# A gated cross-attention and feed-forward kernel: the first batch's value rows cast straight into their stack, W's centring split anew, the context product by parts of W, and the last two tiles reordered

## The chip, the core and the metric

The kernel runs on one core of one Trainium2 chip. The metric is the device time of one execution, in microseconds. Before the change the median of 3 runs is 316.41 us (316.31 to 316.99).

## The reference

x is (4, 2048, 512), the context c is (4, 77, 512), everything float32. LN is a layer norm without weights (eps 1e-5).

```python
scores = einsum('bsd,bvd->bsv', LN(x), c)          # 4 x 2048 x 77
x1  = x  + tanh(g_xattn) * einsum('bsv,bvd->bsd', softmax(scores), c)
Wl  = W + up_aux @ (lora_up @ (lora_down @ down_aux))   # 512 x 512, low-rank part
out = x1 + tanh(g_ffn) * (einsum('bsi,oi->bso', LN(x1), Wl) + b)
```

## The kernel before, in words

The 8192 rows of x are worked as 64 tiles of 128 rows, 16 to a batch. Since LN is linear up to a row's scale, x1's product with W is never made from x1: it is x times W (centred over its input) plus P times (c times W), so that one set of products serves. Tensors of weights are in two parts, a rounded "hi" and a "lo" remainder, each in the type fp32r, and a product is the sum of three such products (hi hi, hi lo, lo hi).

`wc` holds W's two parts (512 columns) and beside them the centred context's columns (77), so that one product of a tile's transposed x (`xT`, hi and lo) gives both x times W and the scores. `x_product` (L502) makes it in halves: h=1 is the wide half with the scores (334 columns), h=0 the other (256). Both halves are 4 chunks of 3 products each. `stacks` holds for a batch the value rows: columns 0 to 511 are tanh(g) c, columns 512 to 1023 the context product tanh(g) c W. Its hi and lo rows stand under each other in the partitions (77 hi rows at 0, 13 lo rows at 77, 13 hi rows again at 96; in a second plane 64 hi rows at 0 and 64 lo rows at 64), in such an order that P's transposed parts (`pT`) times the stack is again the sum of hi and lo products. `p_product` (L518) makes a_ps (P times c, which with x gives x1) and adds P times (c W) to `y_ps`.

For a tile t, in each engine's own order written out by hand (`step`, run for t = 0 to 64 by `all_tiles`):
- TensorE (L540): first chunk of t's wide half, P transpose of tile t-1, the rest of the wide half and half of h=0, `p_product` of t-1, the rest of h=0.
- VectorE (L692): maxima of t, output of t-2, inverse of the exponents' sum of t, x1 rows and mean of t-1, row statistics of t+2, lo parts of P of t.
- ScalarE (L410): hi parts of P of t-1, exponents of t, hi part of x of t+2, probabilities of t, variance of x1 of t-1.
- GpSimd (L300): bias added to x1 of t-1, the two reciprocal roots, lo part of x of t+2.
- SyncE (L232): stores a pair of tiles ("unit") once both are out and loads the unit four further.

The start, before tile 0: TensorE multiplies identities (`stay_busy`, L465) between its first tasks: 12, then the low-rank input product (L473), 4, the context's transposes (L482), the low-rank output product (L566), 6, then the transposes of W rows 0 and 1 with 4 behind each, and at last rows 2 and 3 with the low-rank product L582 into the same banks. W's four blocks of 128 rows are centred first: blocks 0 and 1 on VectorE (L719 to L725), block 2 on ScalarE (L436, L442), block 3 on GpSimd (L330) with the mean of ScalarE. `wc` is then filled by ScalarE (hi, L452) and VectorE (lo, L741), chunk by chunk; the context product (L497, 12 products into a_ps) follows them chunk by chunk. Its result goes to `v_hi` (ScalarE, L358) and `v_lo` (VectorE, L621), and by five SBUF to SBUF copies into the stack: three from SyncE's queue (`stack_hi`, L221) and two from ScalarE's (`stack_lo`, L201, called at L457). TensorE waits for all five (L525) before P's first product. SyncE issues the loads of units 1 and 2 ahead of these copies and those of unit 3 behind them. Batches 1 to 3 are prepared in the same way inside the tile loop, with both kinds of copies on SyncE's queue.

At the end, step 64 has only P's transpose and `p_product` of tile 63 on TensorE; the last unit is stored tile by tile (L270 to L273).

Of the kernel before, what the change touches and what calls it, by code (L numbers as in the profile page):

```python
# [19 lines left out]
def build_kernel(nc, x, xt_in, ctx_in, W, b_gates, low_in, low_out, out):  # L20
# [17 lines left out]
    DMAS = 5  # L38
    assert TB == 2 * HB and V + R <= 96 and D == 512
# [4 lines left out]
    with ExitStack() as stack:  # L44
# [56 lines left out]
        squares = sb("squares", [P, D])  # L101
# [19 lines left out]
        def p_transposed(k):  # L121
            return y_half(k, 0)[:, H:H + P]
# [35 lines left out]
        expd_ok = sem("expd_ok")  # L158
# [6 lines left out]
        def all_tiles(step, prep):  # L165

            for t in range(T + 1):
# [23 lines left out]

        def unit_turn(t, k, ring):

            return t // ring
# [5 lines left out]

        def stack_lo(eng, n):  # L201

            eng.wait_ge(v_lo_ok, 2 * n + 2)
            lo, to = v_lo[:, :].bitcast(F32), stacks[:, n % 2, :, :].bitcast(F32)
            for rows, source in ((to[V:V + R, 0, :], lo[Q:V, :]), (to[Q:P, 1, :], lo[0:Q, :])):
                eng.dma_start(rows, source).then_inc(stacked[n % 2], 16)

        @block.sync
        def _(sp):
# [11 lines left out]
            def stack_hi(n):  # L221
# [5 lines left out]
                sp.wait_ge(v_hi_ok, 2 * n + 2)  # L227
                hi, to = v_hi[:, :].bitcast(F32), stacks[:, n % 2, :, :].bitcast(F32)
                for rows, source in ((to[0:V, 0, :], hi), (to[96:K0, 0, :], hi[Q:V, :]), (to[0:Q, 1, :], hi[0:Q, :])):
                    sp.dma_start(rows, source).then_inc(stacked[n % 2], 16)  # L230
# [18 lines left out]
            sp.dma_start(b_row[:, 0:D], b_gates[0:D].partition_broadcast(P)).then_inc(ld_b, 16)  # L249
            sp.wait_ge(ld_x[0], 16)  # L250
            for u in range(1, 3):
                load_xt(u, u)
                load_x(u, u)
            stack_hi(0)
            load_xt(3, 3)
            load_x(3, 3)
            NU = TB // UNIT
            for u in range(B * NU - 1):
                n, k = u // NU, u % NU
                if n < B - 1:  # L260
# [4 lines left out]
                    if k == NU - 2:  # L265
                        stack_hi(n + 1)
                        stack_lo(sp, n + 1)
# [10 lines left out]
        def _(pool):  # L278
# [15 lines left out]
            def x_lo(t, k):  # L294

                pool.wait_ge(xh_ready, t + 1)
# [3 lines left out]
            def step(t, k):  # L300
# [12 lines left out]
                if t == -2:  # L313
                    first_columns()
                q, a, b = (k + 2) % 4, 0 if real(t + 2) else 1, 2 if real(t - 1) else 1
# [10 lines left out]
            def prep(n, k):  # L326
                pass

            pool.wait_ge(w_nmean_ok, 2)
            pool.tensor_scalar(w_cent[:, 3, :], w_rows[:, 3, :], w_nmean[:, 1:2], None, ALU.add)\  # L330
                .then_inc(w_centred[3], 1)
# [5 lines left out]
        def _(act):  # L337
            act.dma_start(c_rows[:, :], ctx_in[0]).then_inc(ld_ctx, 16)
# [3 lines left out]
            act.dma_start(b_row[:, D:D + 2], b_gates[D:D + 2].partition_broadcast(P)).then_inc(ld_gates, 16)  # L342
# [3 lines left out]
            def ctx_rows_hi(n):  # L346
# [4 lines left out]
                else:  # L351
                    act.wait_ge(stacked[(n - 1) % 2], 16 * DMAS * ((n - 1) // 2 + 1))
# [50 lines left out]
            def variance(t, k):  # L403
# [3 lines left out]
                act.activation(squares[:, :], x1[:, k % 2, :], ACT.Square, bias=x1_nmean[:, k % 2:k % 2 + 1],  # L407
                               scale=D ** -0.5, accum_out=stat[:, s, 2:3]).then_inc(var1_ready, 1)

            def step(t, k):  # L410
                if real(t - 1):
                    p_hi(t - 1, k - 1)
                if switches(t, SWITCH):
# [7 lines left out]
                if real(t - 1):  # L421
# [5 lines left out]

            act.wait_ge(low_mm, 1)
            act.activation(squares[0:LR, :], a_ps[0:LR, :], ACT.Copy, scale=-1.0 / D,
# [3 lines left out]

            for i in range(2):
                act.wait_ge(ld_w[2 + i], 16)
                act.activation(w_cent[:, 2 + i, :], w_rows[:, 2 + i, :], ACT.Copy, scale=-1.0 / D,  # L436
                               accum_out=w_nmean[:, i:i + 1]).then_inc(w_nmean_ok, 1)
# [3 lines left out]
            act.wait_ge(w_nmean_ok, 1)  # L441
            act.activation(w_cent[:, 2, :], w_rows[:, 2, :], ACT.Identity, bias=w_nmean[:, 0:1])\  # L442
                .then_inc(w_centred[2], 1)
            prep(0, TURN)
            act.wait_ge(ld_gates, 16)
            act.activation(tg[:, :], b_row[:, D:D + 2], ACT.Tanh).then_inc(tg_ok, 1)
            x_hi(0, 0)

            act.wait_ge(tg_ok, 1)
# [3 lines left out]
            ctx_rows_hi(0)  # L453
            x_hi(1, 1)
            ctx_product_hi(0)
            act.wait_ge(zeroed, 1)
            stack_lo(act, 0)  # L457
            act.wait_ge(ld_b, 16)
            act.activation(bias_g[:, :], b_row[:, 0:D], ACT.Copy, scale=tg[:, 1:2]).then_inc(biasg_ok, 1)
# [3 lines left out]
        def _(pe):  # L463
# [7 lines left out]
            stay_busy(12)  # L471
# [3 lines left out]
            def prep(n, k):  # L475
# [8 lines left out]
                if k == PRODUCT:  # L484

                    pe.wait_ge(ct_hi_ok, n + 1)
                    if n:
                        pe.wait_ge(ct_lo_ok, n + 1)
                    m = 0
                    for c in range(KC):  # L490
                        for lhs, rhs in ((0, 0), (0, 1), (1, 0)):
                            if n == 0 and lhs == 1 and c == 0:
                                pe.wait_ge(ct_lo_ok, 1)
                            if n == 0 and lhs == 0:

                                pe.wait_ge(w_lo_ok if rhs else w_hi_ok, c + 1)
# [3 lines left out]
                    mm.then_inc(cw_mm, 1)  # L500

# [281 lines left out]
```

## Time and profile before

| | us |
|---|---|
| median of 3 runs | 316.41 |
| the profiled execution | 316.94 |
| its span, first to last instruction | 315.1 |
| TensorE matmul busy | 304.6 (97%) |
| TensorE weight load busy | 290.6 (92%) |
| VectorE busy | 233.0 (74%) |
| GpSimd busy | 224.0 (71%) |
| ScalarE busy | 186.9 (59%) |
| granted TensorE clock, mean | 0.994 |

A busy matmul row counts overlapping, pipelined records, so 97% says that TensorE is nearly always occupied, not that every product is useful: 60 of its 2132 records are identity products of the start. The busy shares cover the whole span; the start and the tail have limits of their own, which are read from the timeline and from the chain of waits. In the chain, each piece stands for the time in which the end of the kernel waited on that work.

### The profile page before, as it was taken

The page shows a single profiled execution, that of the slowest core. Times are in us where ns is not written, and L with a number is a line of the kernel's source. Part 1 is how long each engine was busy: PE and PEld are TensorE (multiplying, and loading weights), DVE is VectorE, ACT ScalarE, POOL GpSimd, SP SyncE. Part 2 cuts the span into 40 slices and gives each one's busy share as a digit, 9 for nine tenths or more (in the row PEclk, how much of TensorE's full clock was granted, in tenths as well). Part 3 has the DMA queues.
Part 4 walks back from the last instruction along what each step waited for, and adds up shares of the span by engine and source line. Part 5 has one row for each costly group of instructions (what it writes and reads, how often), then busy time and mean ns, then how long its engine had stood idle before and what let it go on. Part 6 is the DMA issues. An engine that isn't in the chain of part 4 may idle for free.

```text
span 315.1 us, 6570 instructions
## 1 busy us (share of the span) xinstructions
PE 304.6 (97%) x2132; PEld 290.6 (92%) x2132; DVE 233.0 (74%) x742; ACT 186.9 (59%) x546; POOL 224.0 (71%) x274
## 2 busy tenths in 40 slices
PE   7998999999999999999999999999999999999991
PEld 7878999998999999999899999999899999999981
DVE  3475777797587877798487778788587778777864
ACT  1655665656476565666466566666476665656651
POOL 3435787877577778777578877778488777887752
PEclk9999999999999999999999999999999999999997
DMA  7856254555395455555195565554097555543112
GB/s 217 283 187 199 69 213 158 187 200 203 124 266 191 165 198 200 202 200 203 63 265 196 203 221 202 200 192 175 36 280 241 202 201 200 184 160 129 66 48 89
DMA packets 16588, 56.83 MB, mean 180 GB/s; under 512 B 2116, under 2 KB 2116, under 8 KB 16554
## 3 DMA queue, kind: packets, MB, share of 16 engines
q1 hardware_dynamic: 15724, 54.78, 50.2%
q10 hardware_dynamic: 830, 1.64, 1.5%
q8 instruction: 17, 0.28, 0.4%
q14 instruction: 17, 0.14, 0.1%
HBM read 35.84 MB, written 16.78 MB: 167 GB/s over the span
## 4 chain that ended last, share of the span: by engine, by line
PE 93%; DMA 2%; DVE 1%; POOL 1%; ACT 1%; issue 1%; SPq 1%; POOLq 0%; DVEq 0%; ACTq 0%
PE y_ps L507 64%; PE y_ps L535 9%; PE a_ps L530 9%; PE y_ps L468 3%; PE c_ps L497 3%; PE y_ps L515 2%; DMA stacks<-v_hi 2%; PE a_ps L497 1%; SPq L230 1%; DVE o_sb L687 0%; DVE x L649 0%; POOL x_bias L309 0%; PE y_ps L560 0%; PE c_ps L482 0%; PE a_ps L473 0%
## 5 line engine op out<-in xcount | busy, mean ns | idle before, releaser
L507 PE MATMUL y_ps<-wc,xT 128*128 128x334 f32 (+1 forms) x1536 | 228.1, 302 | 0.0
L507 PEld LDWEIGHTS y_ps<-wc,xT 128*128 128x128 f32 x1536 | 214.4, 189 | 2.1
L309 POOL TENSOR_TENSOR x_bias<-x,bias_g 128x512 f32<-128x512 f32 x63 | 81.4, 1291 | 64.7 <-DVE x L649 64.7
L297 POOL TENSOR_TENSOR xT<-xt_raw,xT 128x512 fp32r<-128x512 f32 x64 | 83.0, 1297 | 0.4 <-ACT xT L378 0.4
L393 ACT ACTIVATE expd<-y_ps,neg_max,rs 128x77 f32<-128x77 f32 x64 | 26.6, 416 | 80.0 <-DVE neg_max L639 80.0
L407 ACT ACTIVATE squares<-x,x_nmean 128x512 f32<-128x512 f32 x64 | 46.4, 725 | 18.3 <-DVE x_nmean L657 18.3
L687 DVE SCALAR_TENSOR_TENSOR o_sb<-y_ps,rs,x_bias 128x512 f32<-128x512 f32 x64 | 48.0, 750 | 2.4 <-POOL rs L322 1.6
L322 POOL TENSOR_TENSOR rs<-stat_eps,half_neg 128x2 f32<-128x2 f32 (+1 forms) x67 | 46.0, 687 | 5.2
L535 PEld LDWEIGHTS y_ps<-stacks,pT 109*128 109x128 f32 (+1 forms) x256 | 39.8, 191 | 5.4
L670 DVE TENSOR_TENSOR pT<-y_ps,pT 13x128 fp32r<-13x128 f32 x64 | 18.6, 291 | 34.5 <-ACT pT L384 34.5
L649 DVE SCALAR_TENSOR_TENSOR x<-a_ps,x_sb 128x512 f32<-128x512 f32 x64 | 43.6, 681 | 0.5 <-PE a_ps L530 0.5
L628 DVE BATCH_NORM_STATS2 bn<-x_sb 128x6 f32<-128x512 f32 x64 | 43.7, 683 | 0.0
L530 PE MATMUL a_ps<-stacks,pT 109*128 109x512 f32 (+1 forms) x128 | 40.4, 397 | 1.7 <-ACT pT L385 1.4
L535 PE MATMUL y_ps<-stacks,pT 109*128 109x256 f32 (+1 forms) x256 | 41.0, 283 | 0.0
L378 ACT ACTIVATE xT<-xt_raw 128x512 fp32r<-128x512 f32 x64 | 39.8, 622 | 0.0
L636 DVE TENSOR_REDUCE s_max<-y_ps 128x1 f32<-128x77 f32 x64 | 14.9, 232 | 21.2 <-PE y_ps L507 20.8
L400 ACT ACTIVATE p_ext<-expd,e_inv 128x154 f32<-128x154 f32 x64 | 26.5, 414 | 0.8 <-DVE e_inv L664 0.6
L384 ACT ACTIVATE pT<-y_ps 96x128 fp32r<-96x128 f32 x64 | 17.0, 266 | 9.6 <-PE y_ps L515 8.7
L530 PEld LDWEIGHTS a_ps<-stacks,pT 109*128 109x128 f32 (+1 forms) x128 | 19.7, 190 | 2.1 <-ACT pT L385 1.6
L320 POOL TENSOR_TENSOR stat_eps<-stat,eps 128x2 f32<-128x2 f32 (+1 forms) x67 | 13.4, 200 | 9.1 <-DVE stat L630 6.5
L673 DVE TENSOR_TENSOR pT<-y_ps,pT 64x128 fp32r<-64x128 f32 x64 | 18.1, 283 | 2.0
L515 PE MATMUL y_ps<-ident,p_ext 128*96 128x128 f32 x64 | 17.4, 271 | 1.4 <-ACT p_ext L400 1.4
(68 smaller groups left out, 196.7 us busy)
## 6 DMA issues: line engine op xcount, KB each, us to landing
x_sb<-in_x SPq DMA_DIRECT2D x32, 512.0 KB, 4.3
xt_raw<-in_xt SPq DMA_DIRECT2D x31, 512.0 KB, 5.2
out<-o_sb SPq DMA_DIRECT2D x31, 512.0 KB, 3.0
stacks<-v_hi SPq DMA_DIRECT2D x4, 308.0 KB
stacks<-v_hi SPq DMA_DIRECT2D x4, 256.0 KB
stacks<-v_lo SPq DMA_DIRECT2D x3, 256.0 KB
w_rows<-in_w SPq DMA_DIRECT2D x2, 256.0 KB, 5.4
w_rows<-in_w ACTq DMA_DIRECT2D x2, 256.0 KB, 6.1
```

Source lines behind the costliest of these rows:

```text
L297: pool.tensor_tensor(xT[:, k % TRING, 1, :, :], xt_raw[:, k % XRING // UNIT, k % UNIT, :, :], xT[:, k % TRING, 0, :, :].bitcast(F32), ALU. ...
L309: pool.tensor_tensor(x1_bias[:, q, :], x1[:, j, :], bias_g[:, :], ALU.add).then_inc(x1b_ready, 1)
L322: pool.tensor_tensor(rs[:, q, a:b], stat_eps[:, q, a:b], half_neg[:, a:b], ALU.pow).then_inc(rs_ready, 1)
L378: act.activation(xT[:, k % TRING, 0, :, :], xt_raw[:, k % XRING // UNIT, k % UNIT, :, :], ACT.Copy)\
L393: act.activation(expd[:, j, 0:V], scores(k), ACT.Exp, bias=neg_max[:, j:j + 1], scale=rs[:, k % 4, 0:1], accum_out=e_sum[:, j:j + 1]).then ...
L407: act.activation(squares[:, :], x1[:, k % 2, :], ACT.Square, bias=x1_nmean[:, k % 2:k % 2 + 1], scale=D ** -0.5, accum_out=stat[:, s, 2:3] ...
L507: mm = pe.matmul(y_half(k, h)[:, 0:n], xT[:, k % TRING, part, c, :], wc[:, c, w, h * H:h * H + n], start=(c == 0 and part == 0 and w == 0) ...
L530: mm = pe.matmul(a_ps[:, :], pT[0:rows[s], k % 2, s, :], stacks[0:rows[s], pair, s, 0:D], start=(s == 0), stop=(s == 1))
L535: mm = pe.matmul(y_half(k, h)[:, 0:H], pT[0:rows[s], k % 2, s, :], stacks[0:rows[s], pair, s, D + h * H:D + (h + 1) * H], start=False, sto ...
L628: dve.bn_stats(bn[:, k % 2, :], x_sb[:, k % XRING, :]).then_inc(bn_ok, 1)
L649: dve.scalar_tensor_tensor(out=x1[:, j, :], in0=a_ps[:, :], scalar=1.0, in1=x_sb[:, k % XRING, :], op0=ALU.mult, op1=ALU.add, accum_out=x1 ...
L687: dve.scalar_tensor_tensor(out=o_sb[:, q, :].rearrange("p (h d) -> p h d", h=2), in0=y_both(k), scalar=rs[:, (k + 3) % 4, 1:2], in1=x1_bia ...
```

## The change

By engine and stage:
- Start, ScalarE: the gates' row is loaded first. tanh and the context's hi rows (`ctx_rows_hi(0)`) come ahead of the low-rank work; then the context transposes' hi part, W block 1's mean, the low-rank output copy, block 2's mean and centring, W's hi parts, x_hi(1), and `first_product_hi`.
- `first_product_hi`: the context product's hi part is cast from PSUM directly into `stacks` at partition 0, and two more casts copy it from there to the second plane and to partition 96. VectorE's lo part for the second plane is also written directly; only the 13 lo rows at partition 77 go by `v_lo` and one copy.
- W blocks 0 and 3 are centred on VectorE, 1 on GpSimd (with ScalarE's mean), 2 on ScalarE. `w_cent` rows are transposed in the order 0, 3, then 1 and 2 chunk by chunk.
- GpSimd also makes the hi part of x tile 0 and `bias_g`.
- TensorE: identity products 12, 4, 6, 4, 4 become 5 and 2. `first_product` takes the two products that need only W's hi part ahead of the one that needs its lo part, one chunk later.
- SyncE: the first 512 columns of the stack's copies (three hi, two lo) go out around unit 1's loads; units 2 and 3 are loaded behind the last copy. Batches 1 to 3 keep their order, through `stack`.
- VectorE: tile 1's row statistics move into step 0, behind the maxima.
- Last two tiles: TensorE has `last_two`; P's transposes go to `c_ps`; ScalarE's variance of tile 62 and VectorE's output of tile 61 move behind other work; `squares` has two buffers.

```diff
-            stack_hi(0)
+            sp.wait_ge(zeroed, 1)
+            sp.wait_ge(v_hi_ok, 1)
+            stack_hi(0, slice(0, D))
             sp.wait_ge(ld_x[0], 16)
+            load_xt(1, 1)
+            load_x(1, 1)
+            sp.wait_ge(v_lo_ok, 1)
+            stack_lo(0, slice(0, D))
+            first_stack_lo()
...
+            pool.wait_ge(w_nmean_ok, 1)
+            pool.tensor_scalar(w_cent[:, 1, :], w_rows[:, 1, :], w_nmean[:, 0:1], None, ALU.add)\
+                .then_inc(w_centred[1], 1)
+            xt_landed(pool, 0, 0)
+            pool.tensor_copy(xT[:, 0, 0, :, :], xt_raw[:, 0, 0, :, :]).then_inc(x0_hi, 1)
...
+                    pool.tensor_scalar(bias_g[:, :], b_row[:, 0:D], tg[:, 1:2], None, ALU.mult).then_inc(biasg_ok, 1)
...
+            def first_product_hi():
+                act.wait_ge(cw_mm, 1)
+                act.wait_ge(zeroed, 1)
+                act.activation(stacks[0:V, 0, 0, D:2 * D], cw_ps(0), ACT.Copy, scale=tg[0:V, 0:1]).then_inc(first_hi, 1)
+                act.wait_ge(first_hi, 1)
+                act.activation(stacks[0:Q, 0, 1, D:2 * D], stacks[0:Q, 0, 0, D:2 * D].bitcast(F32), ACT.Copy)\
+                    .then_inc(first_hi, 1)
+                act.activation(stacks[96:K0, 0, 0, D:2 * D], stacks[Q:V, 0, 0, D:2 * D].bitcast(F32), ACT.Copy)\
+                    .then_inc(first_hi, 1)
...
+                if t == T:
+                    variance(t - 2, k - 2)
...
-                if real(t - 1):
+                if real(t - 1) and t != T - 1:
                     variance(t - 1, k - 1)
...
-            stay_busy(12)
+            stay_busy(5)
...
+            def first_product():
+                pe.wait_ge(ct_lo_ok, 1)
+                for c in range(KC + 1):
+                    if c < KC:
+                        pe.wait_ge(w_hi_ok, c + 1)
+                        for lhs in range(2):
+                            pe.matmul(cw_ps(0), ct[:, lhs, c, :], wc[:, c, 0, 0:D], start=(c == 0 and lhs == 0),
+                                      stop=False)
+                    if c:
+                        pe.wait_ge(w_lo_ok, c)
+                        mm = pe.matmul(cw_ps(0), ct[:, 0, c - 1, :], wc[:, c - 1, 1, 0:D], start=False, stop=(c == KC))
+                mm.then_inc(cw_mm, 1)
...
+            def last_two():
+                a, b = T - 2, T - 1
+                pe.wait_ge(xl_ready, b + 1)
+                pe.wait_ge(out_ready, b - YRING + 1)
+                x_product(b, b, 1, range(0, KC // 2))
+                p_transpose(a, a)
+                x_product(b, b, 1, range(KC // 2, KC))
+                x_product(a, a, 0, range(KC // 2, KC))
+                p_product(a, a)
+                x_product(b, b, 0, range(0, 1))
+                p_transpose(b, b)
+                x_product(b, b, 0, range(1, KC))
+                p_product(b, b)
...
+            pe.wait_ge(w_centred[0], 1)
             for c in range(KC):
+                w_transpose(0, c)
+            stay_busy(2)
+            pe.wait_ge(w_centred[3], 1)
+            for c in range(KC):
+                w_transpose(3, c)
...
+            for c in range(KC):
+                w_transpose(1, c)
+                w_transpose(2, c)
                 pe.matmul(w_bank(c), dn_st[:, c * P:(c + 1) * P], up_st[:, :], start=False, stop=True,
                           skip_group_check=True).then_inc(w_tr, 1)
+            first_product()
+            all_tiles(step, prep, T - 1)
+            last_two()
...
+                if t == 0:
+                    row_stats(1, 1)
-                if real(t - 2):
+                if real(t - 2) and t < T - 1:
                     output(t - 2, k - 2)
...
+                if t >= T - 1:
+                    output(t - 2, k - 2)
...
+            dve.wait_ge(first_hi, 1)
+            dve.scalar_tensor_tensor(out=v_lo[Q:V, D:2 * D], in0=cw_ps(0)[Q:V, :], scalar=tg[Q:V, 0:1],
+                                     in1=stacks[Q:V, 0, 0, D:2 * D].bitcast(F32), op0=ALU.mult, op1=ALU.subtract)\
+                .then_inc(v_lo_ok, 1)
+            dve.scalar_tensor_tensor(out=stacks[Q:P, 0, 1, D:2 * D], in0=cw_ps(0)[0:Q, :], scalar=tg[0:Q, 0:1],
+                                     in1=stacks[0:Q, 0, 0, D:2 * D].bitcast(F32), op0=ALU.mult, op1=ALU.subtract)\
+                .then_inc(first_lo, 1)
```

## Rows read from the trace of the kernel before

**Rows 1.** By windows, whole kernel; columns as its header names them (us, us busy, records).

```profile
...
0.00:4.00 4.00, 2.42 (x11) 2.42 (x12) 0.29 (x1) 0.46 (x1) 2.56 (x10) 1.00 0.44 117
84.00:301.50 217.50, 217.50 (x1547) 210.13 (x1546) 169.40 (x550) 135.38 (x404) 166.78 (x196) 1.00 0.54 187
...
```

**Rows 2.** Chain of waits, 0 to 40 us: start us, us, what.

```profile
...
1.58 5.49 PE y_ps L468 x24
...
10.26 1.54 PE y_ps L468 x12
...
14.46 0.22 PE y_ps L560 x2
...
21.95 5.15 DMA stacks<-v_hi
...
29.61 0.11 PE y_ps L515
...
33.94 0.11 PE y_ps L515
...
```

**Rows 3.** Timeline of the start, 0 to 32 us: start us, us, engine, line, operation.

```profile
...
4.82 0.69 DVE L605 BATCH_NORM_STATS2 c_bn<-c_rows 77x6 f32<-77x512 f32 x1 [3.68 <-DMA c_rows<-in_ctx]
...
6.86 1.24 PE L473 MATMUL a_ps<-low_in_sb 100*68 100x512 f32 x2
...
8.13 0.59 ACT L429 ACTIVATE squares<-a_ps 68x512 f32<-68x512 f32 x1 [3.31 <-PE a_ps L473]
...
9.44 0.62 ACT L436 ACTIVATE w_cent<-w_rows 128x512 f32<-128x512 f32 x1
...
10.85 1.57 POOL L330 TENSOR_SCALAR w_cent<-w_rows,w_nmean 128x512 f32<-128x512 f32 x1 [7.53 <-ACT w_cent L436]
11.13 0.71 ACT L442 ACTIVATE w_cent<-w_rows,w_nmean 128x512 f32<-128x512 f32 x1
...
15.01 2.42 ACT L452 ACTIVATE wc<-y_ps,tg 128x512 fp32r<-128x512 f32 x4 [2.24 <-PE y_ps L582]
...
15.81 2.73 DVE L741 SCALAR_TENSOR_TENSOR wc<-y_ps,tg,wc 128x512 fp32r<-128x512 f32 x4 [3.14 <-ACT wc L452]
...
19.22 3.89 PE L507 MATMUL y_ps<-wc,xT 128*128 128x334 f32 x27
...
19.41 0.69 ACT L358 ACTIVATE v_hi<-a_ps,tg 77x512 fp32r<-77x512 f32 x1 [0.87 <-PE a_ps L497]
...
22.53 0.72 ACT L459 ACTIVATE bias_g<-b_row,tg 128x512 f32<-128x512 f32 x1 [2.43 <-issue]
...
23.16 0.40 ACT L393 ACTIVATE expd<-y_ps,neg_max,rs 128x77 f32<-128x77 f32 x1
...
24.54 0.31 PE L515 MATMUL y_ps<-ident,p_ext 128*96 128x128 f32 x1 [1.43 <-ACT p_ext L400]
...
```

**Rows 4.** Transfers from 0 to 4 us (first row), of the whole kernel (rest).

```profile
...
q1 hardware_dynamic: 142, 0.31, 32.6%
...
out<-o_sb SPq DMA_DIRECT2D x2, 256.0 KB, 2.0
...
low_in_sb<-in_low_in SPq DMA_DIRECT2D x1, 226.6 KB
...
```

**Rows 5.** Timeline of the tail, 297 to 316 us.

```profile
...
303.61 0.28 DVE L673 TENSOR_TENSOR pT<-y_ps,pT 64x128 fp32r<-64x128 f32 x1
304.37 0.24 DVE L636 TENSOR_REDUCE s_max<-y_ps 128x1 f32<-128x77 f32 x1 [0.48 <-PE y_ps L507]
...
306.47 0.72 ACT L407 ACTIVATE squares<-x,x_nmean 128x512 f32<-128x512 f32 x1 [0.36 <-DVE x_nmean L657]
...
308.18 0.70 PE L530 MATMUL a_ps<-stacks,pT 109*128 109x512 f32 x2 [1.37 <-ACT pT L385]
...
309.14 0.68 DVE L649 SCALAR_TENSOR_TENSOR x<-a_ps,x_sb 128x512 f32<-128x512 f32 x1
...
311.85 0.75 DVE L687 SCALAR_TENSOR_TENSOR o_sb<-y_ps,rs,x_bias 128x512 f32<-128x512 f32 x1 [1.23 <-POOL rs L322]
```

More of the change, by code:

```diff
@@ L163, in build_kernel, with all_tiles @@
             sem(n) for n in ("x1_ready", "nmean_ready", "var1_ready", "x1b_ready", "out_ready"))
-        def all_tiles(step, prep):
-            for t in range(T + 1):
+        def all_tiles(step, prep, until=T + 1):
+            for t in range(until):
                 step(t, t)
@@ L219, in load_ctx, with stack_hi, stack_lo, first_stack_lo @@
                 sp.dma_start(c_rows[:, :], ctx_in[n:n + 1].rearrange("o v d -> (o v) d")).then_inc(ld_ctx, 16)
-            def stack_hi(n):
+            def stack_hi(n, cols):
+                hi, to = v_hi[:, cols].bitcast(F32), stacks[:, n % 2, :, cols].bitcast(F32)
+                for rows, source in ((to[0:V, 0, :], hi), (to[96:K0, 0, :], hi[Q:V, :]), (to[0:Q, 1, :], hi[0:Q, :])):
+                    sp.dma_start(rows, source).then_inc(stacked[n % 2], 16)
+            def stack_lo(n, cols):
+                lo, to = v_lo[:, cols].bitcast(F32), stacks[:, n % 2, :, cols].bitcast(F32)
+                for rows, source in ((to[V:V + R, 0, :], lo[Q:V, :]), (to[Q:P, 1, :], lo[0:Q, :])):
+                    sp.dma_start(rows, source).then_inc(stacked[n % 2], 16)
+            def first_stack_lo():
+                sp.wait_ge(v_lo_ok, 2)
+                sp.dma_start(stacks[V:V + R, 0, 0, D:2 * D].bitcast(F32), v_lo[Q:V, D:2 * D].bitcast(F32))\
+                    .then_inc(stacked[0], 16)
+            def stack(n):
                 if n < 2:
@@ L226, in stack_hi @@
                     sp.wait_ge(y_ready, TB * (n - 1))
[L227 to L230, printed above, removed]
+                sp.wait_ge(v_hi_ok, 2 * n + 1)
+                stack_hi(n, slice(0, 2 * D))
+                sp.wait_ge(v_lo_ok, 2 * n + 2)
+                stack_lo(n, slice(0, 2 * D))
             def unit(u):
@@ L432, in _ @@
             act.activation(dn_st[:, :], a_ps[0:LR, :], ACT.Identity, bias=dn_nmean[:, :]).then_inc(dn_hi_ok, 1)
[L434 to L437, printed above, removed]
+            prep(0, TURN)
+            w_mean(1, 0)
             act.wait_ge(low_mm, 2)
             act.activation(up_st[:, :], up_bank(), ACT.Copy).then_inc(up_hi_ok, 1)
-            act.wait_ge(w_nmean_ok, 1)
-            act.activation(w_cent[:, 2, :], w_rows[:, 2, :], ACT.Identity, bias=w_nmean[:, 0:1])\
+            w_mean(2, 1)
+            act.wait_ge(w_nmean_ok, 2)
+            act.activation(w_cent[:, 2, :], w_rows[:, 2, :], ACT.Identity, bias=w_nmean[:, 1:2])\
                 .then_inc(w_centred[2], 1)
[L444 to L449, printed above, removed]
             for c in range(KC):
@@ L738, in _ @@
             dve.wait_ge(tg_ok, 1)
+            ctx_rows_lo(0)
             for c in range(KC):
```

114 lines of the change are left out of this document (49 added, 65 removed).

## The prediction

> **What bounds the kernel now.** I read the view by windows first, then the chain of waits, then the timeline of the start and of the tail. In the tiled middle TensorE has no gap (busy 217.50 of 217.50 us [rows 1]): one tile's P transpose follows the last by 33.94 - 29.61 = 4.33 us, and nothing but TensorE work stands between them [rows 2]. 64 such tiles make 277 us, and the change leaves that work as it is (the edits of `stack`, `stack_landed`, `squares` and the semaphore counts of batches 1 to 3 keep order and operations). So all that can move lies ahead of the second transpose (29.61) and behind the last scores (304.37). The profiled execution took 316.94 us for a span of 315.1; the median of the runs shown is 316.41, so 0.53 is taken off at the end.
>
> The start is a chain through TensorE's own filling. The first twelve identity products (24 records) took 5.49 us, 0.23 each; the next (12 records) 1.54 us, 0.13 each [rows 2]. That is the low and the high of the two levels (1.2 and 2.4 GHz), though the clock column says 1.00 for 0 to 4 us [rows 1]; the durations decide. From 10.26 to 14.46 TensorE worked through 6 + 4 + 4 identity products and the transposes of W rows 0 and 1. Meanwhile rows 2 were centred by 11.13 + 0.71 = 11.84 and rows 3 by 10.85 + 1.57 = 12.42 [rows 3]: at 14.46 the inputs had been waiting 2 us. Behind that come ScalarE's hi casts of W (15.01), VectorE's lo parts (15.81, 2.73 us for four), tile 0's products (19.22), its exponent (23.16), its P transpose (24.54) [rows 3], and the landing of the value stack, 21.95 + 5.15 = 27.10, which released P's first product at 27.2 [rows 2].
>
> **Part 1, the fillers and the W split.** Twelve identity products become five, and 18 later ones become two. The low-rank input product now waits for its load instead. SyncE's queue had moved 0.31 MB by 4.00 us and this load is its first 226.6 KB [rows 4]; the context, begun with it, was in VectorE's hands at 4.82 [rows 3]. I start the product at 4.8. At the high level it took 1.03 of its 1.24 us behind the fillers [rows 3]; at the low level, times 0.23/0.13, 1.9: done 6.7. ScalarE then, by its pitches in [rows 3]: row sum and centring 1.3 (8.13 to 9.44), context transposes' hi 0.5, the first row mean of W 0.6: 9.2. The low-rank output product runs behind the context's transposes, 7.2 to 9.1 at the low level, so ScalarE's copy of it runs 9.2 to 9.8, the second mean to 10.6, the centring of rows 2 (0.71) to 11.4, with semaphores 11.5. GpSimd centres rows 1 from 9.3 in 1.57: 10.9. VectorE does rows 0 and 3 by 10.4. TensorE's last transposes start at 11.5 in place of 14.46: 2.9 gained. The tanh (0.2) and the context's hi rows move ahead of this, into the time before 6.7 in which ScalarE only waited. Cost of the lost fillers: by [rows 2] the rate doubled behind 5.49 us of unbroken work. Here unbroken work starts near 6.8, so it may be 12.3 before it doubles. Then W rows 3's transposes, and the first of the last ones, run at half rate: 0.3 for each. Bounds 0 and 0.6; I take 0.4. Sum: 2.5.
>
> GpSimd gets the first x cast (row nearest: 512 elements at 1.57 us or less), the low part, two copies and the bias: 10.9 + 0.7 to 1.6 + 1.3 + 0.8 + 1.6 = 15.3 to 16.2. Its next duty, tile 0's statistics, comes from VectorE at 18.54 - 2.5 + 0.9 = 16.9, so this is hidden, with 0.7 to 1.6 to spare.
>
> **Part 2, the context product.** Behind W's last lo part there were two products, now there is one. 27 records with 334 or fewer columns took 3.89 us, 0.14 each [rows 3]; for 512 columns that is 0.2. The pace of the rest is VectorE's (2.73 us for four), which stays. Tile 0's products start at 19.22 - 2.5 - 0.2 = 16.5.
>
> **Part 3, the direct casts.** Before, 19.22 to 24.54 was 5.32 us, with ScalarE busy issuing two copies and then on the bias (22.53, 0.72) while the maxima were ready: exponent at 23.16 [rows 3]. Now, counted from the products' start: ScalarE's hi cast at 0.2 to 0.9 as before (19.41), two more casts of 0.6 up to 2.2; VectorE's two lo parts 0.95 to 2.4 (0.7 each by 2.73/4); maxima 2.4 to 2.9; exponent 2.95; its sum 3.55. VectorE has put tile 1's statistics in between (one pass of 0.7 and its aggregate, 0.9; 2.9 to 3.8), so the inverse waits 0.3: 4.0; probabilities 4.05 to 4.45; transpose 4.5. So 4.5 in place of 5.3: 0.8 gained. Bounds: 1.1 if the two casts and lo parts are short, 0 if each new instruction costs 0.3 more.
>
> **Part 4, the stack's landing.** The five old copies landed together; of the new six all but one, of 13 rows, go out from 9 us on. SyncE's queue is longer by five issues before unit 1's loads end (12.1 becomes 13), and units 2 and 3 stand behind the last copy, at about 19; they are wanted at tiles 4 and 6, 10 us on. The last copy is issued at 16.5 + 1.7 = 18.2 (VectorE's first lo part), and by the 2.0 us that a 256 KB store takes from issue to landing [rows 4] it is in by 21, while P's first product is due at 16.5 + 4.5 + 2.3 = 23.3. So the wait is gone, and the next transpose follows by 4.33 + 0.15 of refill, not by 29.61 - 24.54 = 5.07: 0.6 gained. If the copy takes 5.15 us from its issue, like the old ones, it comes at 24.2: 0.9 lost, which leaves bounds of -0.3 and 0.6.
>
> Start in all: 2.5 + 0.2 + 0.8 + 0.6 = 4.1.
>
> **Part 5, the last two tiles.** The scores of tile 63 are finished before tile 62's second half, but VectorE is at tile 62's P until 303.61 + 0.28 = 303.9, so the maxima come at 303.9 in place of 304.37 [rows 5]; the exponent, the inverse and the transpose follow at 304.5, 305.1 and 305.8. The hi copy of P stood behind the variance of tile 62 (306.47 + 0.72), that is 307.19; with the variance behind it, it can start at 306.15. VectorE is through tile 62's x1 at 306.25 and does the lo parts by 307.05. P's last product: 307.1, not 308.18. VectorE's output of tile 61 takes the place that tile 62's had before x1 of tile 63, so 309.14 becomes 307.85, and the last output 311.85 becomes 310.55: 1.3. Three stores now leave within 3.5 us (before, two); I take 0.1 for it. Sum: 1.2; bounds 0.6 (another engine's order binds) and 1.4.
>
> **A rule and a row on the last copy.** The row has 5.15 us from issue to landing, for copies that left together [rows 2]. The Trainium skill (DMA: Bandwidth & Descriptors, Anatomy of one DMA, fitted there for GpSimd's path) puts a transfer at about 2.0 us plus its bytes over 436 GB/s; for these 13 rows of 2 KB that is an estimate of 2.1 us, a landing near 21 and no wait, where the row gives 24.2 and 0.9 us lost. The sum above rests on the store's row, the case of the 5.15 us is rival B.
>
> **Rivals.** A: the clock stays at 1.2 GHz through W's transposes and the context product. TensorE would then need 4 x 0.93 from 11.9, and 12 products at 0.25 x 1.8 = 0.45 behind them, 5.3: end at 20.9 without a rise, near 19 with one midway. Tile 0 starts at about 19 and not 16.5: 2.5 lost, 313.7. For it: from 6.8 on the engine has gaps that the fillers closed, at the waits for W's rows. Against: they are short, and from 11.5 on there are none. Chance 0.13.
> B: the last copy is late (part 4), or the longer SyncE queue delays unit 1: 0.9 to 1.2 lost, 312.3. Chance 0.08.
> C: the tail does not shorten, because tile 61's output and the three stores take the place of what went: 1.2 lost, 312.4. Chance 0.06.
> D, the other side: the clock is low until P's first product. Tile 0's 27 records (3.89 us at 19.22 [rows 3]) and the 15 behind the transpose then cost double: A without its midway rise, 4.4, and 3.5 to 5.5 more, less 1.0 of waits that they fill: 318.5. It decides against the change once the clock rises later than some 23 us. TensorE is unbroken for over 5.49 us long before that. Chance 0.05.
> E: the change doesn't do what it says: W rows 2 wait for a load that now comes later (the gates' row goes first on ScalarE's queue), and 14.46 hardly moves. It would take a load 3 us later than at 9.44; the result is then 314.5 to 316.5. Chance 0.03.
>
> **How the numbers follow.** 316.94 - 4.1 - 1.2 = 311.6 for an execution like the profiled one, less 0.53 is 311.1. With the unlikely ends of the terms all good (no clock cost, 0.3 more in part 3, 0.2 more in the tail) it is 310.2. Forecast 311.1 with 0.65; its own range 310.2 to 312.2. B and C lie inside 312.5, A at 313.7; the range of 8 in 10 is 310.2 to 313.8. Within 0.2% of 316.41 (about what a measurement of this kernel can tell from no change) is 315.8 to 317.0: 0.03, from E. Slower 0.05, from D. Faster 0.92.
>
> **What would show it.** After: the last W transposes near 11.6, ScalarE's W casts at 12.1 to 12.7, tile 0's products at 16.5, its exponent 3 us behind them, its transpose at 21.0; P's first product with no DMA as its releaser; the second transpose at 25.5 and 4.33 us a tile from there; at the end 1.2 us less between the last tile's start and the end. Records of the W transposes and context products at twice the old pitch would mean A; a wait for the stack, B; a wait of GpSimd's low part ahead of tile 0 or 1 would mean that part 1's cover was too thin. The forecast is wrong if the middle is not 4.33 us a tile.

## The result, and the profile after

The changed kernel takes 312.82 us (median of 4 runs, 312.59 to 313.07) against 316.36 for the kernel before: a ratio of 0.9894, 95% interval 0.9876 to 0.9912, 3.5 us faster. Forecast were 311.1 us and, with 8 chances in 10, 310.2 to 313.8. The profiled execution went from 316.94 to 313.07, its span from 315.1 to 311.3, and the two traces show where: the second P transpose starts at 27.35, before at 29.61 [rows 2], 2.26 us earlier; the last output starts at 308.01, before at 311.85 [rows 5], 3.84 earlier. The start gave 2.26 us where 4.1 were forecast, the tail the other 1.58 where 1.2 were.

The chain of waits of the changed kernel (start us, us, what; L631 is the low-rank output product, L626 the transposes of W, L508 identity products, L647 the low-rank product in W's banks, L543 and L547 the context product, L563 P's transpose):

```profile
...
1.15 5.08 DMA c_rows<-in_ctx
...
7.72 0.78 PE c_ps L522 x4
8.50 1.90 PE y_ps L631 x2
10.40 1.05 PE y_ps L626 x4
11.45 0.85 PE y_ps L508 x4
12.30 1.28 PE y_ps L626 x6
...
14.01 0.43 PE y_ps L626 x2
...
14.86 0.27 PE y_ps L626 x2
...
15.36 0.22 PE y_ps L626 x2
...
18.13 0.47 PE a_ps L547 x2
...
27.35 0.11 PE y_ps L563
...
31.68 0.11 PE y_ps L563
...
```

It answers to [rows 2]. The head of the chain is no longer filling but a load: the context's, 5.08 us. Behind it TensorE works without a wait up to 18.60, at half rate for most of it: two transposes take 0.43 us up to 14.86, 0.27 and 0.22 from there. So the rate doubles at about 15 us; in the kernel before it was 7. The middle is as it was, 31.68 - 27.35 = 4.33 us a tile.

The timeline of its start, lines that answer to [rows 3] (L631 is again the low-rank output product):

```profile
...
5.25 1.97 PE L513 MATMUL a_ps<-low_in_sb 100*68 100x512 f32 x2 [1.16 <-DMA low_in_sb<-in_low_in]
...
6.25 0.69 DVE L671 BATCH_NORM_STATS2 c_bn<-c_rows 77x6 f32<-77x512 f32 x1 [5.10 <-DMA c_rows<-in_ctx]
...
8.43 0.30 PEld L631 LDWEIGHTS y_ps<-low_out_sb 50*68 50x68 f32 x2 [0.16 <-DMA low_out_sb<-in_low_out]
...
14.04 0.69 ACT L497 ACTIVATE wc<-y_ps,tg 128x512 fp32r<-128x512 f32 x1 [1.65 <-PE y_ps L647]
...
14.76 2.92 DVE L812 SCALAR_TENSOR_TENSOR wc<-y_ps,tg,wc 128x512 fp32r<-128x512 f32 x4 [0.87 <-ACT wc L497]
...
18.43 3.90 PE L555 MATMUL y_ps<-wc,xT 128*128 128x334 f32 x27
...
21.42 0.42 ACT L423 ACTIVATE expd<-y_ps,neg_max,rs 128x77 f32<-128x77 f32 x1 [0.79 <-DVE neg_max L705]
...
22.82 0.31 PE L563 MATMUL y_ps<-ident,p_ext 128*96 128x128 f32 x1 [0.49 <-ACT p_ext L430]
...
```

The context is in VectorE's hands at 6.25, before at 4.82. The low-rank output's load is late too: L631 at 8.43 waits for it. W's first hi cast comes 0.97 earlier than before, tile 0's products only 0.79 earlier. From these to P's transpose it is 22.82 - 18.43 = 4.39 us (before 5.32), and to the next transpose 4.53 (before 5.07).

The tail (timeline), against [rows 5]:

```profile
...
301.42 0.24 DVE L702 TENSOR_REDUCE s_max<-y_ps 128x1 f32<-128x77 f32 x1
...
304.55 0.70 PE L581 MATMUL a_ps<-stacks,pT 109*128 109x512 f32 x2
...
305.28 0.69 DVE L715 SCALAR_TENSOR_TENSOR x<-a_ps,x_sb 128x512 f32<-128x512 f32 x1 [0.18 <-PE a_ps L581]
...
308.01 0.75 DVE L753 SCALAR_TENSOR_TENSOR o_sb<-y_ps,rs,x_bias 128x512 f32<-128x512 f32 x1 [0.58 <-POOL rs L350]
```

Less the 2.26 of the start, the last tile's maxima come 0.69 earlier, P's last product 1.37, the last x1 rows 1.60, the last output 1.58. From there to the end of the span it is 3.27 us (before 3.25): the three stores, which now leave closer together, cost nothing.

Why the context is late shows in the transfers between 1.6 and 5.4 us. Changed kernel (first row all packets, then SyncE's queue q1 and ScalarE's queue q10: packets, MB, share of 16 engines), and then the kernel before:

```profile
...
DMA packets 342, 0.41 MB, mean 108 GB/s; under 512 B 156, under 2 KB 156, under 8 KB 342
...
q1 hardware_dynamic: 128, 0.27, 37.4%
q10 hardware_dynamic: 214, 0.14, 14.4%
...
```

```profile
...
DMA packets 448, 0.87 MB, mean 229 GB/s; under 512 B 42, under 2 KB 42, under 8 KB 448
...
q1 hardware_dynamic: 292, 0.57, 58.1%
q10 hardware_dynamic: 156, 0.30, 23.1%
...
```

The gates' row goes to 128 partitions, so it is 128 packets of 8 bytes. Put first, they are most of the 156 packets under 512 B, and ScalarE's queue moves 0.14 MB in the time in which it moved 0.30. SyncE's queue, where these packets do not stand, is slower as well, 0.27 MB for 0.57. Why is not shown: no run changed the number of packets and left the rest as it was.

### The profile page after: what moved, and what is told of

Same layout as the page of the kernel before. It is cut to its first block, busy times and chain, and to the rows that moved or that the text cites. A ratio compares the mean times of both kernels' runs of the same rounds, so it can differ in the third digit from the quotient of the medians.

```text
span 311.3 us, 6483 instructions
## 1 busy us (share of the span) xinstructions
PE 302.0 (97%) x2086; PEld 286.1 (92%) x2086; DVE 235.0 (75%) x743; ACT 187.5 (60%) x546; POOL 226.5 (73%) x276
## 4 chain that ended last, share of the span: by engine, by line
PE 94%; DMA 2%; DVE 1%; ACT 1%; issue 0%; POOLq 0%; ACTq 0%; POOL 0%; DVEq 0%
PE y_ps L555 66%; PE y_ps L586 10%; PE a_ps L581 10%; PE c_ps L531 3%; PE y_ps L563 2%; DMA c_rows<-in_ctx 2%; PE y_ps L626 1%; PE y_ps L631 1%; PE a_ps L543 1%; PE c_ps L522 1%; PE y_ps L647 0%; PE a_ps L547 0%; PE y_ps L508 0%; DVE o_sb L753 0%; DVE v_lo L818 0%
## 5 line engine op out<-in xcount | busy, mean ns | idle before, releaser
L414 ACT ACTIVATE pT<-y_ps 96x128 fp32r<-96x128 f32 x62 | 16.5, 266 | 9.6 <-PE y_ps L563 8.7
L415 ACT ACTIVATE pT<-y_ps 64x128 fp32r<-64x128 f32 x62 | 16.6, 268 | 1.5
L563 PE MATMUL y_ps<-ident,p_ext 128*96 128x128 f32 x62 | 16.8, 271 | 0.5 <-ACT p_ext L430 0.5
```

## The experiments

Each kernel ran in 4 to 6 executions beside 8 to 11 of the kernel before on the same chip; ratios are to those.

### Which load stands first

```diff
+            act.dma_start(c_rows[:, :], ctx_in[0]).then_inc(ld_ctx, 16)
             act.dma_start(b_row[:, D:D + 2], b_gates[D:D + 2].partition_broadcast(P)).then_inc(ld_gates, 16)
-            act.dma_start(c_rows[:, :], ctx_in[0]).then_inc(ld_ctx, 16)
```

> The changed kernel with the context's load ahead of the gates' row on ScalarE's queue. Theory 1 (the head of the start's chain is the context's landing, late because 128 eight-byte rows of the gates stand ahead of it): it lands at 4.8 to 5.2 us and not 6.25; the context's transposes then wait for the low-rank input product only, 7.2 in place of 7.72, and all behind them comes 0.5 us earlier: 312.3. Theory 2 (what binds the start is TensorE's low rate until 14.83): the landing moves, the start of tile 0's products does not by more than 0.2: 312.7. Rival: the gates now land late and hold up tanh and ScalarE's low-rank work: slower by up to 0.5.

Measured: 313.17 us, ratio 0.9890 (0.9877 to 0.9904), no different from the changed kernel. The context did come early, at 4.70, but the chain now had the low-rank output's load at its head:

```profile
...
1.78 6.58 DMA low_out_sb<-in_low_out
...
```

It landed at 8.36, and L631 started at 8.41, in the changed kernel at 8.43. Theory 1 saw only one of the two loads: in the changed kernel both stand behind the gates' row and both are late, and the second alone holds L631 where it was.

### More identity products at the head

```diff
-            stay_busy(5)
+            stay_busy(8)
```

> The changed kernel with 8 identity products at the head in place of 5 (they end at 5.24, when the low-rank input is there anyway). Theory 2 (the low rate until 14.83 binds): the rate doubles at 7 to 11.5 us, block 0's transposes, the low-rank output product and the fillers shrink, tile 0's products start 1.0 to 1.5 us earlier: 311.3 to 311.8. Theory 1 (the context's landing binds): no change, 312.8.

Measured: 312.41 us, ratio 0.9876 (0.9853 to 0.9898), but its six runs lie between 311.70 and 313.98. The profiled one (311.70) has in its chain:

```profile
...
1.15 5.29 DMA c_rows<-in_ctx
...
12.33 0.41 PE y_ps L626 x2
...
14.34 0.93 PE a_ps L543 x4
...
16.66 0.48 PE a_ps L547 x2
...
```

The rate had doubled by 7.9 (the low-rank input product, up to 7.15, still took 1.98, the output product 1.07). Each product of W and of the context takes 0.23, and tile 0's products start at 16.97 in place of 18.43. That is the 1.0 to 1.5 us of theory 2. The other runs say that this is not got each time.

### All the old identity products

```diff
-            stay_busy(5)
+            stay_busy(12)
...
+            stay_busy(4)
             prep(0, TURN)
...
+            stay_busy(6)
             pe.wait_ge(w_centred[0], 1)
...
-            stay_busy(2)
+            stay_busy(4)
...
+            stay_busy(4)
             pe.wait_ge(w_centred[1], 1)
```

> The changed kernel with all the old identity products (12, 4, 6, 4, 4 in place of 5 and 2). If the fewer fillers gave the start its gain, as the prediction has it (2.5 us): 315.3. Theory 2 (what their removal gave in issue time it took back by the low rate): the rate doubles at 7.1, tile 0's products start at 18.9 to 19.2 and not 18.43: 313.2 to 313.6. Rival (all of the start's gain comes from the new split and order of W): 312.8.

Measured: 313.33 us, ratio 0.9892 (0.9877 to 0.9906). In the profile the context product ends at 19.19, with the changed kernel's five and two at 18.60. So by the profiles, leaving out 23 of 30 identity products gave 0.6 us and not 2.5: what they had cost in time came back as half rate. The whole runs don't tell even the 0.6 from nothing (0.9892 against 0.9894).

### The old tail

The edit takes back `last_two`, P's transposes in `c_ps`, and the moved variance and output.

```diff
-            all_tiles(step, prep, T - 1)
-            last_two()
+            all_tiles(step, prep)
...
-                if real(t - 1) and t != T - 1:
+                if real(t - 1):
                     variance(t - 1, k - 1)
```

> The changed kernel with the last two tiles as they were (order of TensorE, ScalarE's variance, VectorE's output of tile 61, P's transposes in their old bank). The traces put 1.6 us on the tail (3.84 less at the last output, 2.26 of it from the start): 314.4. Prediction's term: 1.2, so 314.0. Rival C of the prediction (the tail gives nothing): 312.8.

Measured: 315.23 us, ratio 0.9957 (0.9945 to 0.9969). The tail's part is 0.9957 - 0.9894 = 0.0063, 2.0 us, with about 0.7 us of uncertainty in the two intervals; its trace gives 1.8 at the last output (309.81 against 308.01), 0.22 of it from a rate that doubled a little later. That agrees with 1.6 us; rival C is out.

### The gates' row third

```diff
-            act.dma_start(b_row[:, D:D + 2], b_gates[D:D + 2].partition_broadcast(P)).then_inc(ld_gates, 16)
             act.dma_start(c_rows[:, :], ctx_in[0]).then_inc(ld_ctx, 16)
             act.dma_start(low_out_sb[:, :], low_out).then_inc(ld_out, 16)
+            act.dma_start(b_row[:, D:D + 2], b_gates[D:D + 2].partition_broadcast(P)).then_inc(ld_gates, 16)
```

> The changed kernel with the gates' row third on ScalarE's queue, behind the context and the low-rank output's load, ahead of W's blocks. Theory 1b (the 128 rows of 8 bytes hold this queue for some 3 us, and whatever stands behind them is late: the context at 6.25 in the changed kernel, the low-rank output at 8.4 where the context goes first): the context is there at 4.8 and the low-rank output by 6; the context's transposes start at 7.2, the output product at 7.7 in place of 8.43; with an unchanged clock tile 0's products start 0.7 earlier: 312.2. Theory 2 alone (the rate's rise at 14.83 binds): under 0.3 of it comes through, 312.7.

Measured: 315.02 us, ratio 0.9957 (0.9941 to 0.9973), 2 us worse than the changed kernel where 0.6 better was expected. My expectation had left out who waits for the gates. The timeline:

```profile
...
4.64 0.69 DVE L671 BATCH_NORM_STATS2 c_bn<-c_rows 77x6 f32<-77x512 f32 x1 [3.50 <-DMA c_rows<-in_ctx]
...
7.88 0.20 ACT L478 ACTIVATE tg<-b_row 128x2 f32<-128x2 f32 x1 [3.05 <-DMA b_row<-in_b_gates]
...
8.81 0.57 ACT L482 ACTIVATE squares<-a_ps 68x512 f32<-68x512 f32 x1
...
```

The context came early, as expected. But tanh is the first of ScalarE's tasks and waited 3.05 us for the gates, until 7.88, and with it all of ScalarE's low-rank work (L482, at 8.81; in the changed kernel at 7.26). VectorE and TensorE followed: TensorE waited 1.31 us for W's rows, up to 12.50, and still took 0.43 us for two transposes of W at 16.17.

### The same with eight identity products

The edits of the last and of the second experiment together.

> As the last, with 8 identity products at the head in place of 5. Theories 1b and 2 together (late loads and the low rate each cost; both gone, ScalarE's and VectorE's work on W is what is left, as the prediction had it): the rate doubles by 8.5 us, tile 0's products start at 16.3 to 16.8 (changed kernel 18.6), and all runs show it: 310.8 to 311.3. If the loads alone matter: 312.2; if the clock alone: 311.5.

Measured: 314.95 us, ratio 0.9944 (0.9923 to 0.9965), where 310.8 to 311.3 was expected. By windows (us; busy us and records of TensorE, its weight loads, VectorE, ScalarE, GpSimd; then granted clock, DMA share, GB/s):

```profile
...
8.00:12.00 4.00, 0.74 (x7) 0.55 (x5) 1.79 (x4) 3.90 (x10) 0.91 (x1) 1.00 0.85 313
12.00:16.00 4.00, 3.62 (x14) 3.02 (x15) 3.89 (x6) 2.19 (x4) 3.91 (x6) 0.50 0.92 275
16.00:20.00 4.00, 4.00 (x15) 2.51 (x14) 2.99 (x5) 1.89 (x3) 2.09 (x3) 0.65 0.42 144
...
```

With ScalarE late, TensorE was busy for 0.74 of the 4 us from 8 to 12, and from 12 to 16 its clock is 0.50: a rate that has risen falls again. W's last transposes, from 12.4 on, and the first five of the context product's twelve products (16.90 to 18.98) then ran at 1.2 GHz.

### The first stack's product half by copies

```diff
-                act.activation(stacks[0:V, 0, 0, D:2 * D], cw_ps(0), ACT.Copy, scale=tg[0:V, 0:1]).then_inc(first_hi, 1)
...
+                act.activation(v_hi[:, D:2 * D], cw_ps(0), ACT.Copy, scale=tg[0:V, 0:1]).then_inc(first_hi, 1)
...
+                sp.wait_ge(first_hi, 1)
+                stack_hi(0, slice(D, 2 * D))
+                sp.wait_ge(v_lo_ok, 2)
+                stack_lo(0, slice(D, 2 * D))
```

> The changed kernel with the product half of the first stack made as before: through v_hi and v_lo, and five copies from SyncE's queue. Prediction's parts 3 and 4 (the landing of these copies held P's first product, 0.6 us and more): they land 5 to 5.5 us behind their issue at 19.4 to 21, that is 25.5 to 26.5, P's first product waits 0.5 to 1.4 us: 313.5 to 314.2. Rival (the landing is hidden, since tile 0's transpose and 15 products take until 25.07): 312.5, a little faster, as VectorE has one lo part less ahead of the maxima.

Measured: 313.20 us, ratio 0.9908 (0.9878 to 0.9938), runs from 311.96 to 315.12; too wide to tell. Its profile (which had the rate double at about 15, like the changed kernel's) tells more:

```profile
...
19.36 2.17 SPq L225 DMA_DIRECT2D stacks<-v_hi  x3
...
21.57 1.34 SPq L231 DMA_DIRECT2D stacks<-v_lo  x2
...
24.73 0.71 PE L574 MATMUL a_ps<-stacks,pT 109*128 109x512 f32 x2
...
```

The last two copies were issued from 21.57 on, and no wait for a transfer stands before P's first product at 24.73 (in the chain its two parts take 0.62 in place of 0.46, so at most 0.16 of a wait). In its chain the next transpose stands at 27.10, in the changed kernel's at 27.35.

### The old order of the context product

```diff
+                for c in range(KC):
+                    for lhs, rhs in ((0, 0), (0, 1), (1, 0)):
+                        if lhs == 0:
+                            pe.wait_ge(w_lo_ok if rhs else w_hi_ok, c + 1)
```

> Kernel of e6 with the context product's order as before (hi hi, hi lo, lo hi for each part of W, two products behind the last lo part). Prediction's part 2: one product of 0.23 us more behind W's last lo part, tile 0's products 0.2 later than in e6: e6 + 0.2. Rival (TensorE's backlog from the W transposes sets the pace, not VectorE's lo parts): e6 + 0.

Measured: 314.20 us, ratio 0.9935 (0.9915 to 0.9954), within e6's spread (313.68 to 315.43), since here too the clock fell and rose again. In its chain the 12 products stand in one piece, 16.58 to 19.35, 0.23 each, with no wait for a lo part: TensorE came late from W's transposes. So the order was worth nothing here. With W's transposes at the high rate it wasn't tried alone. Two traces bear on it: from W's last transposes to tile 0's products it is 4.44 us in e3 (14.58 to 19.02) and 4.76 in the kernel before (14.46 to 19.22), where TensorE waited for the first lo part. Whether the order or the somewhat earlier lo part saved these 0.3 is open.

### Loads in the old order, tanh where the gates have landed

```diff
-            act.dma_start(b_row[:, D:D + 2], b_gates[D:D + 2].partition_broadcast(P)).then_inc(ld_gates, 16)
             act.dma_start(c_rows[:, :], ctx_in[0]).then_inc(ld_ctx, 16)
             act.dma_start(low_out_sb[:, :], low_out).then_inc(ld_out, 16)
             load_w(act, 2)
             load_w(act, 3)
+            act.dma_start(b_row[:, D:D + 2], b_gates[D:D + 2].partition_broadcast(P)).then_inc(ld_gates, 16)
...
             w_mean(1, 0)
+            act.wait_ge(ld_gates, 16)
+            act.activation(tg[:, :], b_row[:, D:D + 2], ACT.Tanh).then_inc(tg_ok, 1)
+            ctx_rows_hi(0)
```

> The changed kernel with the loads in the old order (context, low-rank output, W's blocks, then the gates' row) and tanh and the context's hi rows behind ScalarE's first row mean of W, so that nothing waits for the gates at the head of ScalarE's order. Identity products as in the changed kernel (5 and 2). Theory 1c (what made e5 late was tanh at the head of ScalarE's order, waiting for gates that landed at 7.88; the early context is good in itself): the context's transposes at 7.0, W's last transposes at 12.4 in place of 13.15, 0.7 gained with the rate still low until 14 or so: 312.1. Rival (the rate alone counts; with 5 and 2 it may rise at 15 or fall back): 312.8 to 315.

Measured: 311.84 us, ratio 0.9874 (0.9848 to 0.9901), five runs from 311.61 to 312.21 and one of 314.38. The chain:

```profile
...
0.72 4.32 DMA low_in_sb<-in_low_in
...
7.57 1.90 PE y_ps L631 x2
...
12.28 0.41 PE y_ps L626 x2
...
16.62 0.49 PE a_ps L547 x2
...
25.85 0.11 PE y_ps L563
...
```

TensorE has no gap from 5.08 to 12.23, the low-rank output product is 0.9 earlier, W's last transposes start at 12.28 in place of 13.15, and the rate doubled with them; tile 0's products start at 16.93, the second transpose of P is at 25.85, 1.5 ahead of the changed kernel. The edit has a price: tanh and the context's hi rows (9.32 to 10.33) now stand in ScalarE's work on W, which ends at 12.18.

### More identity products, loads as in the changed kernel

```diff
-            stay_busy(5)
+            stay_busy(8)
...
-            stay_busy(2)
+            stay_busy(4)
...
                 w_transpose(3, c)
+            stay_busy(4)
```

> The changed kernel with more identity products: 8 at the head in place of 5, 4 in place of 2 behind block 0's transposes, and 4 more behind block 3's. Theory 2b (the gaps between TensorE's tasks at the start leave the rate low, or let it fall back as at 12.20 in e6, and that is what spreads e2's runs from 311.7 to 314.0): the rate rises by 8.5 and stays, the W transposes and the context product run at full rate, tile 0's products start at 17.4 to 17.7 in place of 18.6, and all runs lie within 0.5 us: 311.7. Rival (the fillers cost what they give, as in e3): 312.8.

Measured: 314.73 us, ratio 0.9949 (0.9930 to 0.9968): neither theory 2b nor its rival, but worse than both. TensorE's timeline, and then the windows (only the first columns matter: TensorE's busy us, and the clock behind GpSimd's):

```profile
...
5.23 1.07 PE L513 MATMUL a_ps<-low_in_sb 100*68 100x512 f32 x2
8.11 0.64 PE L522 MATMUL c_ps<-ident,c_cent 77*128 77x77 f32 x4 [1.80 <-DVE c_cent L678]
...
```

```profile
...
4.00:8.00 4.00, 2.27 (x9) 1.20 (x7) 1.30 (x4) 2.58 (x6) 0.00 (x0) 1.00 0.90 272
8.00:12.00 4.00, 3.89 (x13) 2.13 (x14) 3.77 (x9) 2.96 (x8) 2.08 (x2) 0.54 0.87 313
...
```

The rate rose early, at about 5, so that the low-rank input product took 1.07 us and was done at 6.3. The context came at 6.63, its transposes at 8.11, after 1.80 us of waiting; the clock is down in the stretch behind that wait (0.54 for 8 to 12), and the identity products behind W's blocks 0 and 3 ran at half rate but for the last of them (16 records in 1.71 + 1.37 us). From W's last transposes on (15.63) it was high again, too late to help. In e2's profile, with the same head, the rate rose only after the low-rank input product and TensorE's wait for the context was 0.79 us; there it did not fall. So identity products alone do not hold the rate in every execution; the late load has to go too.

### Both

The edits of the last two together.

> Both edits together (e9's order of loads and of ScalarE, e10's identity products). If both theories hold: tile 0's products start at 16.9 to 17.3, 311.2, the best of these kernels, with runs within 0.5 us. If only the rate counts: as e10. If the two get in each other's way (ScalarE's order binds at 12.4 in any case): as e10 too.

Measured: 311.25 us, ratio 0.9840 (0.9819 to 0.9861), four runs from 310.61 to 311.62. This interval lies below the changed kernel's and e10's; it overlaps e9's.

```profile
...
4.00:8.00 4.00, 4.00 (x15) 2.16 (x14) 2.62 (x6) 1.68 (x4) 0.00 (x0) 1.00 1.02 319
8.00:12.00 4.00, 3.09 (x24) 2.55 (x24) 3.22 (x7) 3.87 (x10) 2.38 (x3) 1.00 0.82 270
12.00:16.00 4.00, 4.00 (x24) 2.92 (x23) 3.98 (x6) 3.13 (x6) 3.93 (x4) 1.00 0.79 240
...
```

```profile
...
25.86 0.11 PE y_ps L563
...
```

No stretch of 4 us has TensorE under 3.09 busy (its longest wait is 0.91 us), the clock stays, and P's second transpose is at 25.86, where the forecast had it at 25.5. Against e9 it is no earlier in the profile. What it may add is that the runs agree: one of e9's six is late, none of e11's four and e12's five.

### The same with the product half by copies

> Kernel of e11 with the first stack's product half by copies, as in e7. In e7 the profile had the copies landed when P's first product was due (24.73) and the second transpose at 27.10, 0.25 ahead of the changed kernel, but its runs spread over 3 us with the clock. Theory (the direct casts cost VectorE a second lo part ahead of the first maxima, 0.4 us, and save no wait once the first half is copied early): the second transpose 0.25 ahead of e11's, 311.0. Prediction's parts 3 and 4 (the direct casts are what took the landing off the path): slower than e11 by 0.5 to 1.4, 311.8 to 312.6.

Measured: 311.35 us, ratio 0.9833 (0.9810 to 0.9855), runs from 310.87 to 311.62: the same time as e11. In the chain:

```profile
...
23.30 0.65 PE a_ps L574 x2
...
25.61 0.11 PE y_ps L559
...
```

P's first product follows the 15 products before it (0.65 for two, against 0.46 in e11, so at most 0.2 of a wait), and the second transpose is 0.25 ahead of e11's. The whole runs don't show that 0.25: by the two intervals e12 is 0.2 us ahead of e11 with about 1.0 of uncertainty, which by itself leaves room for a gain of the direct casts of 0.5. It is the two profiles that leave none, with at most 0.2 of a wait.

## Why the prediction was right, point by point, and where its terms were off

The direction and the range of 8 in 10 were right; the time was 1.7 us too low and lies outside the forecast's own range of 310.2 to 312.2. The start gave 1.84 us less than forecast, the tail 0.38 more, and the last 0.28 is the 0.53 taken off at the end: the changed kernel's profiled execution lay only 0.25 above its median. So the miss is part 1's, and the tail hid some of it.

**Part 1** (forecast 2.5, measured 0.8 at tile 0's products). The step that failed is "The context, begun with it, was in VectorE's hands at 4.82. I start the product at 4.8", together with "the low-rank output product runs behind the context's transposes, 7.2 to 9.1". The diff put the gates' row ahead of the context on ScalarE's queue, and I had not priced that at all; only rival E named the gates, and for W's rows. The context came at 6.25, the low-rank output's load at about 8.4, and the output product ran 8.50 to 10.40, 1.30 us late.

Two more pieces were mis-sized. The sum let W's last transposes wait for the centrings alone. But behind the output product TensorE had 2.75 us of its own work at the low level (10.40 to 13.15), while rows 2 were centred by 11.67 + 0.72 = 12.39: even with the loads on time that is 9.1 + 2.75 = 11.85 and not 11.5. And the lost fillers' "I take 0.4" was 0.6: from W's last transposes to tile 0's products it took 5.28 us, against 4.65 in e9 at the high rate (12.28 to 16.93). Together 1.3 + 0.35 + 0.2 is the 1.9 us by which tile 0's products missed 16.5.

The forecast's moment for the clock, "it may be 12.3 before it doubles", took the 5.49 us of unbroken work from [rows 2] as enough. Here TensorE was busy without a gap from 7.72 and the rate doubled at about 15; in e5 it was busy without a gap from 4.90 to 11.18 and the rate did not rise at all in that time. What decides the moment stays open. So a part of rival A happened: its place (W's transposes at half rate) was right, its price of 2.5 us was not.

e9 (loads) and e2's profile (rate) each start tile 0's products 1.5 us earlier than the changed kernel, and e11, with both, does too: they do not add up, since in all three W's last transposes start at about 12.3. P's second transpose is then at 25.85, 3.8 of the 4.1 forecast for the start. What keeps 12.3 from 11.5 is in e9 and e11 tanh and the context's hi rows, which the prediction had put ahead of 6.7 and which now take ScalarE's time behind 9.3. Rival E did not come: the centring of W's rows 2 was done before TensorE's own order came to them.

**Part 2** (0.2, measured 0): TensorE came behind W's transposes with a backlog of hi products, so VectorE's last lo part was not what ended last. e8's chain, one piece of 12, says the same. At the high rate the new kernel may gain 0.3 (e3, above).

**Parts 3 and 4** (0.8 and 0.6, measured 0.93 and 0.54): the sizes were right, the reason half wrong. By e7 and e12 the direct casts themselves give nothing (0.25 lost in the profile, no difference in the runs). What is left to have paid is what came with them. The bias and the issue of two copies leave ScalarE, which had the exponent wait until 23.16 [rows 3]; it now starts 2.99 us behind tile 0's products, before 3.94, and that is the whole gain of part 3. And the first half of the stack goes out 7 to 10 us earlier, so that what is left lands in time even as five copies. No run took these two apart. Rival B is out. Its price came from the 5.15 us of [rows 2]; in e12 the last two copies were issued at 20.06 and later and were in by 23.3, 3.2 us at most. The Trainium skill (DMA: Bandwidth & Descriptors, Anatomy of one DMA) with its 2.0 us and a part by bytes was nearer than that row, which timed copies of twice the columns, with the others of the stack ahead in the queue; no run here shows the landing of the 13 rows itself, only that nobody waited for it.

**Part 5** (1.2, measured 1.58): the stores' 0.1 was not paid, and P's last product came 0.3 earlier than worked out. e4 agrees with the size (2.0 us, with 0.7 of uncertainty).

**Rival D** did not come in any run of the changed kernel, but a milder form exists: in e6, e8 and e10 the clock fell back before tile 0, and in e6 it was low until 18.98. Even there the kernels stayed ahead of the kernel before (ratios 0.9944, 0.9935, 0.9949), as the tail's 1.6 us held. **GpSimd's cover** in part 1 held: its bias ended at 14.57 + 1.57 = 16.14, tile 0's statistics came at 18.50. (Its sum used 18.54 where the trace of the kernel before has 18.45; nothing hangs on the 0.09.)

## What to carry to other kernels

When a diff moves a load to the head of a queue, price what stands behind it, also where it has few bytes: here 1 KB in 128 packets made two loads late. Then ask which engine's first task waits for it, because moving it back alone (e5) can cost more than it gives. Identity products at a kernel's start are not free to remove or to add: e3, with all of them, took the same time as the changed kernel with seven. What gave time was to close TensorE's longest wait at its cause (a late load) first, and to fill what was left (e9, e11); filling alone gave 1.5 us in one profile (e2) and cost 1.7 in another kernel (e10). When several edits come together, find by one experiment each which of them pays: here the casts that gave the change its name did not.

## What the runs showed of the hardware that I had not expected

- 128 packets of 8 bytes at the head of ScalarE's queue went with a context 1.4 us later (6.25 for 4.82) and a low-rank output's load that landed at about 8.4, also with the context ahead of them (8.36 in e1). ScalarE's queue moved 0.14 MB in 3.8 us where it had moved 0.30, SyncE's 0.27 where it had moved 0.57. In e5 the gates' row itself, 1 KB, took 6.15 us to land.
- The rate that has risen can fall back within the start: behind 1.80 us of waiting in e10, and after 0.74 busy us out of 4 in e6. It did not fall over waits of 0.79 and 1.00 us in e2's profile and 0.91 in e11's. It rose at about 5 us in e10, between 7.1 and 7.9 in e2's profile and at 15 in the changed kernel, with heads of 8, 8 and 5 identity products, and the runs of e2 differ by 2.3 us: the same program does not get the same moment each time. Why e2's runs fall in groups was not settled.
- The clock column shows 1.00 from the start up to the first fall, also while products take twice their time (two transposes of W in 0.43 us between 12 and 15 us in the changed kernel, column 1.00); a low rate at the start is read from the durations alone.
